# Shared conv2 products copied into two PSUM banks, where the products that use them accumulate

## The reference

```
h      = relu(bn1(conv1(x)))                # 1 tap, 128 -> 128 channels
h      = bn2(conv2(h))                      # 17 taps along the nodes, padding 8
x_conv = relu(h + x)
s      = x @ w_se.T + b_se                  # 3 numbers per node
A      = exp(-|s_n - s_m|^2) * adj
msg    = relu(x @ w_msg.T + b_msg)
x_nmp  = A @ msg
gi, gh = [x_conv, x_nmp] @ w_ih.T + b_ih, x @ w_hh.T + b_hh
r, z   = sigmoid(gi_r + gh_r), sigmoid(gi_z + gh_z)
out    = layernorm(x + (1 - z) * tanh(gi_n + r * gh_n) + z * x)
```

## Time and profile before

| | us |
|---|---|
| median of 3 runs | 304.82 (304.56 to 306.04) |
| the profiled execution's own time | 304.77 |
| its span | 302.5 |
| TensorE busy | 293.3 (97%) |
| TensorE weight loads | 237.0 (78%) |
| VectorE busy | 247.2 (82%) |
| ScalarE busy | 164.5 (54%) |
| GpSimd busy | 22.6 (7%) |

### The profile page before, as it was taken

The page is one execution under the profiler, slowest core; times in us unless marked ns, Lnnn a source line. Parts: engine busy times, 40 slices in busy tenths (PEclk is TensorE's granted clock), DMA queues, the critical chain, the costliest instruction groups (busy, mean ns, idle before and its releaser), DMA issues.

```text
span 302.5 us, 4661 instructions
## 1 busy us (share of the span) xinstructions
PE 293.3 (97%) x1409; PEld 237.0 (78%) x1409; DVE 247.2 (82%) x668; ACT 164.5 (54%) x355; POOL 22.6 (7%) x49
## 2 busy tenths in 40 slices
PE   7999999999999999999999999999999999999991
PEld 5787788688888788888887878888888878888871
DVE  2799999889779969758959969858968997945793
ACT  3876744697856222477865314268883622225444
POOL 3100000000000410000000150000000060000122
PEclk9999999999999999999999999999999999999996
DMA  7502435432103311811203230532211221240002
GB/s 251 210 0 73 140 141 173 138 105 70 37 31 93 122 72 45 256 56 60 69 35 104 75 133 35 166 147 69 69 35 35 69 103 63 55 128 0 18 19 104
DMA packets 12257, 27.23 MB, mean 90 GB/s; under 512 B 1363, under 2 KB 2133, under 8 KB 12117
## 3 DMA queue, kind: packets, MB, share of 16 engines
q1 hardware_dynamic: 11956, 26.03, 26.0%
q10 hardware_dynamic: 288, 1.05, 1.0%
HBM read 22.88 MB, written 4.19 MB: 90 GB/s over the span
## 4 chain that ended last, share of the span: by engine, by line
PE 82%; DVE 9%; DMA 3%; issue 2%; ACT 1%; POOL 1%; SPq 0%; POOLq 0%; DVEq 0%; ACTq 0%
PE bank L328 79%; DMA z<-wcv_dram 3%; PE bank L546 2%; PE bank L381 1%; DVE first L1169 1%; DVE H L1135 1%; POOL rstd L892 1%; DVE x L987 1%; DVE x_lo L1020 1%; DVE H L1150 0%; DVE xr L1371 0%; DVE xr L1376 0%; ACT hn L812 0%; DVE w_hl L995 0%; DVE xr L1117 0%
## 5 line engine op out<-in xcount | busy, mean ns | idle before, releaser
L328 PE MATMUL bank<-V_hi,cw_hi 128*128 128x512 f32 x160 | 69.6, 435 | 0.2 <-DVE cw_lo L1007 0.2
L328 PE MATMUL bank<-V_hi,cw_lo 128*128 128x512 f32 x160 | 63.8, 399 | 0.0
L328 PE MATMUL bank<-V_lo,cw_hi 128*128 128x512 f32 x160 | 63.6, 397 | 0.0
L328 PE MATMUL bank<-x_hi,w_hl 128*128 128x512 f32 x120 | 44.3, 410 | 0.1
L328 PEld LDWEIGHTS bank<-V_hi,cw_lo 128*128 128x128 f32 x160 | 30.0, 188 | 7.8
L328 PE MATMUL bank<-c_hi,w_hl 128*128 128x512 f32 x96 | 35.5, 397 | 0.5 <-DVE c_lo L1154 0.5
L328 PEld LDWEIGHTS bank<-V_hi,cw_hi 128*128 128x128 f32 x160 | 30.2, 189 | 7.1 <-issue 0.3
L328 PEld LDWEIGHTS bank<-V_lo,cw_hi 128*128 128x128 f32 x160 | 30.2, 188 | 6.6
L328 PE MATMUL bank<-m_hi,w_hl 128*128 128x512 f32 x96 | 35.2, 399 | 0.0
L682 ACT ACTIVATE m_hi<-bank 128x512 fp32r<-128x512 f32 x16 | 9.6, 599 | 32.9 <-PE bank L328 32.9
L328 PEld LDWEIGHTS bank<-x_hi,w_hl 128*128 128x128 f32 x120 | 22.6, 188 | 5.4 <-DVE x_lo L1020 0.5
(11 more groups left out here) (145 smaller groups left out, 586.5 us busy)
## 6 DMA issues: line engine op xcount, KB each, us to landing
adj<-adj_dram SPq DMA_DIRECT2D x16, 512.0 KB, 4.7
x<-xt_dram SPq DMA_DIRECT2D x16, 256.0 KB, 3.2
xn<-xn_dram SPq DMA_DIRECT2D x16, 256.0 KB, 4.7
out_dram<-xn SPq DMA_DIRECT2D x15, 256.0 KB, 2.1
xr<-xt_dram SPq DMA_DIRECT2D x12, 256.0 KB, 3.7
xn<-wcv_dram SPq DMA_DIRECT2D x1, 1024.0 KB, 7.5
xr<-xt_dram ACTq DMA_DIRECT2D x1, 768.0 KB, 6.1
EF<-wsm_dram SPq DMA_DIRECT2D x1, 512.0 KB, 3.2
```

The costliest lines, as they stand in the source:

```text
L328: return nc.tensor.matmul(out, lhs, rhs, start=start, stop=stop, skip_group_check=True)
```

## The change

Side products no longer meet the shared one on VectorE. ScalarE copies the shared product out of `shared_bank` (bank 6) into both `side_bank`s (7 and 0), and the two products that use it are accumulated there by TensorE on top of it (no matmul of theirs has start=True). So that this adds up, the taps of odd phases and the third tap sum are stored negated. `product` is gone. ScalarE's `half` reads the first two sums with bn2's scale and shift, VectorE's `base` adds x to them, and `conv_sum` is one instruction for each phase. A bank goes over from the pair sums to conv2, so that there is one `nmp_bank` (bank 1). The order on every engine is rewritten around this: products F1 and E3 change places, gathers go in pairs, turn_rows(g, 1) stands behind D3. The setup has one more warm matmul, on bank 0.

```diff
 PRODUCTS = [
     (H3, S0123, True), (D2, S02, True), (D3, S13, False),
-    (E1, S01, True), (F0, 0, True), (F1, 1, False),
-    (E3, S23, False), (F2, 2, False), (F3, 3, False),
+    (E1, S01, True), (F0, 0, True), (E3, S23, False),
+    (F1, 1, False), (F2, 2, False), (F3, 3, False),
 ]
+SHARED = (0, 3, 5)
+SIDES = (1, 2)
+PHASES = (4, 6, 7, 8)
...
-        nmp_bank = [bank[1], bank[0]]
-        conv2_bank = [bank[6], bank[7]]
+        nmp_bank = bank[1]
+        shared_bank, side_bank = bank[6], [bank[7], bank[0]]
...
             # SyncE, first group
             load_x(0, 0)
             load_x(0, 2)
-            sp.wait_ge(prod_used, 2)
             load_x(0, 1)
             load_adj_late(0, 2)
-            sp.wait_ge(cw_ready, 7)
+            sp.wait_ge(cw_ready, 6)
             load_x(0, 3)
...
+            sp.wait_ge(msg_done, 8)
             for s in range(2):
-                sp.wait_ge(prod_used, 4 + 2 * s)
                 load_xs(1, s)
...
             # TensorE, gather
                 if b == 0:
-                    pe.wait_ge(lr_ready, 2 * g + (1 if first else 2))
-                elif b == 2:
                     if first:
                         pe.wait_ge(lr_ready, 2)
                     else:
                         pe.wait_ge(y_ready, 4 * g)
                 elif b % 2 == 0:
-                    pe.wait_ge(m_ready, 4 * g + pair - 1)
+                    pe.wait_ge(m_ready, 4 * g + pair)
...
             # TensorE, conv2
-                if n == 1 and not first:
-                    pe.wait_ge(msg_ready, 8 * g + 8)
-                if n >= 2:
-                    if (n - 2) % 3 == 0:
-                        pe.wait_ge(s_ready, 3 * g + (n - 2) // 3 + 1)
-                    else:
-                        pe.wait_ge(prod_used, 6 * g + (n - 2) - (n - 2) // 3)
+                if n in (1, 2):
+                    pe.wait_ge(copy_ready, 6 * g + n)
+                elif n >= 4:
+                    pe.wait_ge(copy_ready, 6 * g + (3, 4, 4, 5, 6)[n - 4])
+                if n in SHARED:
+                    out = shared_bank
+                elif n in SIDES:
+                    out = side_bank[SIDES.index(n)]
+                else:
+                    out = side_bank[PHASES.index(n) % 2]
...
-                    last = three(conv2_bank[n % 2][:, :], cw_hi[:, w, :], cw_lo[:, w, :], vh, vl, t == 0,
+                    last = three(out[:, :], cw_hi[:, w, :], cw_lo[:, w, :], vh, vl, n in SHARED and t == 0,
                                  t == TG + extra - 1)
...
             # TensorE, order in the mixing stage: first group
                 elif n == 3:
                     turn_rows(0, 1, True)
-                    gather(0, 0, True)
                 elif n == 4:
                     distances(0, 1)
+                    gather(0, 0, True)
                     gather(0, 1, True)
...
             # later groups
                         distances(g, 0)
-                        pe.wait_ge(msg_ready, 8 * g + 7)
+                    elif n == 2:
+                        pe.wait_ge(exp_ready, 8 * g + 4)
                         turn_rows(g, 1)
-                    if n == 3 and not first:
+                    elif n == 3:
                         distances(g, 1)
-                    if n >= 1 and not first:
+                        gather(g, 0, first)
+                        gather(g, 1, first)
+                    elif n in (4, 6, 8):
+                        gather(g, n - 2, first)
                         gather(g, n - 1, first)
...
             # TensorE, setup
+            pe.wait_ge(msg_ready, 2)
+            warm(side_bank[1], 1, 4)
             mix_stage(0, True)
...
             # ScalarE
+            def shared(g, j, side):
+                act.wait_ge(conv2_done, NP * g + SHARED[j] + 1)
+                if j == 0 and side == 0:
+                    act.wait_ge(msg_ready, 8 * g + 8)
+                elif j == 1:
+                    act.wait_ge(p_ready, 2 * g + side + 1)
+                elif j == 2:
+                    act.wait_ge(t_ready, 4 * g + side + 1)
+                nc.scalar.activation(side_bank[side][:, :], shared_bank[:, :], ACT.Copy).then_inc(copy_ready, 1)
+
+            def half(g, side, first):
+                act.wait_ge(conv2_done, NP * g + SIDES[side] + 1)
+                if side == 0 and not first:
+                    act.wait_ge(vb_ready, 4 * g)
+                P1 = P1_first if first else P1_later
+                nc.scalar.activation(P1[:, side, :], side_bank[side][:, :], ACT.Identity, bias=v(SH2),
+                                     scale=v(SC2)).then_inc(p_ready, 1)
...
             # ScalarE, order, first group, up to the copies of E1
                     slot_high(E1, E_all[:, 1], elow_ready, 1)
-                    shared(g, 0, first)
+                    shared(g, 0, 0)
+                    shared(g, 0, 1)
                     slot_high(F0, F_one, slot_diff, 1)
                     operands(0, 0, True)
                     tap_hi(0)
-                    tap_hi(1)
+                    sum_hi(3)
+                    half(g, 0, first)
                     act.wait_ge(hhr_ready, 1)
                     weights(g, 0)
                     weights(g, 1)
-                    slot_high(F1, F_one, slot_diff, 2)
+                    slot_high(E3, E_all[:, 3], ehigh_ready, 1)
+                    half(g, 1, first)
+                    tap_hi(1)
                     weights(g, 2)
                     weights(g, 3)
-                    sum_hi(3)
-                    slot_high(E3, E_all[:, 3], ehigh_ready, 1)
-                    shared(g, 1, first)
+                    slot_high(F1, F_one, slot_diff, 2)
+                    shared(g, 1, 0)
+                    shared(g, 1, 1)
                     operands(g, 1, True)
...
             # ScalarE, order, later groups
+                shared(g, 0, 0)
+                late_hi(g, 2)
+                shared(g, 0, 1)
+                weights(g, 0)
+                weights(g, 1)
+                late_hi(g, 3)
+                weights(g, 2)
+                weights(g, 3)
+                half(g, 0, first)
+                operands(g, 1)
+                half(g, 1, first)
+                shared(g, 1, 0)
+                shared(g, 1, 1)
+                weights(g, 4)
+                sums_hi(g, 0)
...
             # VectorE
+            def base(g, c, first):
+                dve.wait_ge(p_ready, 2 * g + c % 2 + 1)
+                P1 = P1_first if first else P1_later
+                TT(inner(c), grid(P1[:, c % 2, :]), phase(x, c), ALU.add).then_inc(t_step, 1)
 
             def conv_sum(g, c, first):
+                dve.wait_ge(conv2_done, NP * g + PHASES[c] + 1)
+                dve.wait_ge(t_step, 4 * g + 4)
+                STT(inner(c), grid(side_bank[c % 2][:, :]), v(SC2 if c < 2 else NSC2), inner(c), ALU.mult,
+                    ALU.add).then_inc(t_ready, 1)
...
             # VectorE, order, later groups, up to the second pair sum
+                late_lo(g, 2)
+                mask(g, 0)
+                late_lo(g, 3)
+                residual(prev, NC - 1)
+                mask(g, 1)
+                norm_stats(prev, 0)
+                mask(g, 2)
+                norm_stats(prev, 1)
+                base(g, 0, first)
+                mask(g, 3)
+                norm_mean(0)
+                norm_mean(1)
+                norm_stats(prev, 2)
+                base(g, 2, first)
+                norm_stats(prev, 3)
+                base(g, 1, first)
+                norm_mean(2)
+                norm_mean(3)
+                base(g, 3, first)
+                normalise(prev, 0)
+                normalise(prev, 1)
+                sums_lo(g, 0)
+                mask(g, 4)
+                mask(g, 5)
+                normalise(prev, 2)
+                conv_sum(g, 0, first)
+                mask(g, 6)
+                normalise(prev, 3)
+                sums_lo(g, 1)
```

More of the change, by code:

```diff
@@ L599, in gru_stage, with warm @@
                         messages(g + 1, 2 * k + 1)
-            def warm(n, blocks):
+            def warm(out, n, blocks):
                 rows = ones_r[:, :].rearrange("p (o d) -> p o d", o=1).broadcast_to([P, blocks, P])
                 for _ in range(n):
-                    mm(bank[7][:, 0:blocks * P], ones_r[:, :], rows, start=True, stop=True)
+                    mm(out[:, 0:blocks * P], ones_r[:, :], rows, start=True, stop=True)
             pe.wait_ge(warm_ready, 2)
-            warm(WARM[0], 4)
+            warm(side_bank[0], WARM[0], 4)
             pe.wait_ge(first_loaded, 16)
             conv1_first(0)
-            warm(WARM[1], 2)
+            warm(shared_bank, WARM[1], 2)
             for k in (1, 2, 3):
@@ L654, in set_bias @@
                 if b < 2:
-                    act.wait_ge(*((m_ready, 4 * g - 1), (prod_used, 6 * g - 1))[b])
+                    act.wait_ge(*((m_ready, 4 * g), (t_ready, 4 * g - 1))[b])
                 else:
@@ L762, in mix_stage @@
-                shared(g, 2, first)
```

(84 more changed lines are left out.)

146 lines of the change are left out of this document (45 added, 101 removed).

## The result

Four executions of the changed kernel took 309.11, 310.26, 310.67 and 311.34 us, median 310.47, beside 304.87 for the kernel before: a ratio of 1.017 (95% interval 1.013 to 1.022). The forecast was 308.5 in 306.8 to 311.0. The profiled execution is the one of 309.11 us, with a span of 307.3 us and a mean granted clock of 0.995; in the other three the mean was 0.988 to 0.990. The second and the fourth experiment show that a fall of the clock accounts for most of what these three took more.

A forecast was written before the change was run, and what follows sets the result against it. TensorE, busy 97% of the span, was taken as the bound. First stage +2.7 us and three later groups +0.9 made 3.6 on 304.77, 308.4; with 0.1 for the edge at product 1, 308.5, range 306.8 to 311.0.

The forecast's parts named there:

- The stall at product 1: First group: D2 waits for ScalarE's copy of H3's result, starting near 21.5 and not 18.97; 2.5 us (2.2 to 2.7).
- The stall at product 4: First group: F0 waits for its copy behind eight others in ScalarE's queue; 0.95 us (0.5 to 1.4).
- The rest of the first group: First group: rows(1) and base(0) delayed on VectorE, with small later waits; 0.1 us (0 to 1.0).
- The two old gaps: End of first group: TensorE's gaps of 0.64 and 0.23 us go, with c_lo ready before TensorE asks; -0.87 us.
- Later groups, product 1: Each later group: the copy before D2 is covered by turn and distances with 0.1 us to spare; cost 0.
- Later groups, gather 2: Each later group: gather 2 waits for sums_lo(0) behind normalise on VectorE; 0.3 us a group (0 to 0.8).
- The rival: TensorE's clock falls in the 2.5 us stall at D2, priced at 1.5 us; total 309.8, chance 0.27.
- The argument against the rival: Tail idle, where the clock fell, was never ended by new work; the first-group stall has work on both sides.
- The prediction's other basis: Kernel's end: granted clock falls to 0.50 within the slice 1.5 us after TensorE's last matmuls; the stall is longer.
- No collision at gather 2: Later groups: rival without the wait for sums_lo(0) at gather 2; total 307.6, chance 0.12.
- dearer copies: Every group: rival with copies at 0.76 us, adding 0.2 at product 1, gather 2 at 0.8; 310.6, chance 0.08.
- VectorE as the bound of the first stretch: First group: rival where the copies' stalls are slack and lighter VectorE work ends it earlier; 303.9, chance 0.05.

The follow-up runs named there:

- The second: Changed kernel plus nine 512-column matmuls into a free bank between keep_bias and D2 of the first group; 309.15 us (1.0137).
- the fourth experiment: Changed kernel with sums_lo(0) of the later groups moved ahead of normalise(1) on VectorE; 309.23 us (1.013).
- the fifth experiment: Changed kernel with the first group's copy for D2 (keep_bias in bank 3) and E1's first copy moved up ScalarE's queue; 306.60 us (1.005).
- the eighth: the sixth's kernel with, in the first group, sums_lo(0) ahead of conv_sum(0), sums_hi(2) and sums_lo(2) ahead of gate-weight preparation; 304.35 us (0.9987).
- the sixth: Changed kernel with both early copies in the first group and sums_lo(0) ahead of normalise(1) in later groups; 305.54 us (1.0018).
- The first experiment: Kernel before with one wait more: D2 of the first group waits for ScalarE's old read of H3's result; 307.75 us (1.0094).
- the seventh: Kernel before without conv_sum's four additions of x, four VectorE instructions fewer in each group; 303.33 us (0.9955).
- the ninth experiment: the eighth's kernel plus six one-column memsets in each VectorE mixing stage, restoring 668 instructions; 304.52 us (0.9987).

## Why the prediction was right, and where it was not

*The stall at product 1, 2.5 us:* shown, 2.54. The cause was as read, the copy's place in ScalarE's queue: moving it (with keep_bias) takes 2.6 us off the profiled time, and the wait alone adds 2.74 to the kernel before. The copy took 0.58 us for the 0.60 taken. The Trainium skill (ScalarE: Activation LUTs, section "Step-by-step: what each stage is for") holds writes to PSUM to be faster than those to SBUF; ScalarE's 512-wide reads of a bank into SBUF take 595 ns here and the copies between banks 581. The difference has the rule's sign, but it is 14 ns of the 250 by which it could have changed the sum, and the two are not the same function.

*The stall at product 4, 0.95:* 1.05 us.

*The rest of the first group, 0.1:* too small. The sums at gathers 2 and 6 had been worked out to margins of 0.35 and -0.1 us; measured 0.37 and 0.18. rows(1) started at 26.10, not 25.6, and the addition of x at 37.53, 0.95 us after VectorE was ready for it. In the fifth experiment the same wait for x passes on to gather 2; in the eighth, with sums_lo(0) ahead of conv_sum(0) and x landing 0.25 sooner than in the sixth, the wait at the gather is gone.

*The two old gaps, -0.87:* right in size, wrong in half of its reason. I gave both TensorE's lateness and VectorE's lighter load. The first experiment has the lateness without the lighter load, and the gap stays; the seventh has the lighter load without the lateness, and it is gone. So the lighter load is enough and the lateness is not. In the changed kernel both are there, and its order on VectorE is new as well; which part each has there is not shown; the last c_lo is done at 60.09 and asked for at 61.74, the margin of 1.65 that had been worked out. 0.87 us is all the change got back from TensorE's waits for 15 us of VectorE's work.

*Later groups, product 1, 0:* right: no wait for the copy in any pass, as the table of waits has only the two of the first group.

*Later groups, gather 2, 0.3 each:* 0.35 by the fourth experiment. The pass is 0.41 longer; the other 0.06 is not traced.

*The sum.* For the profiled execution the first group ends 3.71 later: 2.54 + 1.05 + 0.37 + 0.18 - 0.87 = 3.27, and 0.27 of start (the first ten matmuls took 4.63 us, not 3.90, and VectorE's and ScalarE's rows up to the copy are 0.27 later with it, as EF at 19.12 for 18.85), and 0.15 for the first step after each copy's gap, which takes 0.31 and not 0.235: 3.69. The start is not the change's doing: the first experiment, which is the kernel before up to D2, has the same 4.63. The added warm matmul, taken at 0.05, starts 0.33 before H3, but D2 waits for ScalarE and so hides it. Three passes add 1.23. That is 4.9 for 4.8 in the span, where I had forecast 3.7; outside the span 0.45 went away that I had left unchanged, which hid part of the miss: 304.77 + 4.8 - 0.45 = 309.1.

*The clock.* Here the likeliest case was not the common one, and this is what puts the median outside the forecast's own 307.3 to 309.6 and near the top of the range given. The forecast of 308.5 took the clock to hold through the stall, and in the profiled execution it did. In the other three the mean clock is lower by 0.005 to 0.007 and the time longer by 1.2 to 2.2 us. The rival, 309.8 with a chance of 0.27, read a price of 1.5 us from the kernel's start and put 1.3 into its sum; it is 1.51 by the rows of the fourth experiment and 1.3 by the second. With it the median is 309.1 + 1.4 = 310.5; the 2.2 of the longest execution is more than the clock explains. That the start gave the right price is partly luck. The profile's granted clock reads 1.00 at the start in every run, so the low level there is read from the matmuls' steps alone, and the same ten matmuls took 3.90 us before but 4.63 in the changed kernel and in the first experiment, from which the price would have come out at 2.3. The argument against the rival, that there is work on both sides of the stall, did not hold: in the fourth experiment the clock fell some 0.5 us after TensorE had resumed.

Why the clock fell in some executions and not in others is not settled: the first experiment had an idle of 2.52 us at the same place, and its four runs lie within 0.4 us. The prediction's other basis was the tail, where the clock fell 1.5 us after TensorE's last matmul. That was one value of many. In the changed kernel the last matmuls end at 300.96 and in the eighth experiment's at 296.02, and the first slices whose granted clock (the third number from the end) is below 1.00 come 3.2 and 4.2 us later; in the profiled executions of all eleven kernels it is between 1.5 and 4.2 us. An idle of 2.4 us lies inside that spread.

```profile
304.20:304.40 0.20, 0.00 (x0) 0.00 (x0) 0.15 (x1) 0.00 (x0) 0.00 (x0) 0.66 0.00 0
```
```profile
300.20:300.40 0.20, 0.00 (x0) 0.00 (x0) 0.00 (x0) 0.00 (x0) 0.00 (x0) 0.82 1.08 420
```

The Trainium skill (TensorE: Matmul & The Clock Gate, section "What's actually happening") says that the chip's look at activity runs freely and does not begin with the kernel, so that the same kernel meets it at different points; the two outcomes of one gap in the same program and the spread in the tails agree with that, but no run here shows the cause.

*The other rivals.* No collision at gather 2 and dearer copies: refuted by the passes. VectorE as the bound of the first stretch: refuted by the first experiment, where a stall on TensorE costs its whole length, and by the seventh, where 2.4 us less of VectorE's work per group shorten the first group by 1.03.

## What to carry to other kernels

When an operation becomes a condition for the bounding engine, price it by its place in the queue of its own engine and not by its duration alone: here 0.6 us of copy cost 2.5, and with the copy moved up the stall was gone. Before trading work away from an engine that does not bound the kernel, ask what waits for it: 15 us less on VectorE was worth 0.9 on TensorE. Mending one stall can uncover the next: F0's gain was lost at gather 2 until sums_lo(0) was moved as well. An idle of some 2.4 us on TensorE is to be priced at its length and, in part of the executions, some 1.5 us more: by their times 3 of 4 of the changed kernel's and 4 of 6 of the fourth experiment's, but none of 4 in the first.

## What was not expected of the hardware

The time outside the span was 2.15 to 2.36 us for the kernel before and its copy with one wait more, and 1.74 to 1.92 for the changed one, all its variants and the seventh experiment's. The difference is some 0.45 us, and its cause is open: the ninth experiment excludes the number of VectorE's instructions executed. About two thirds of the eighth version's lead over the kernel before are this, and not its schedule.
